# Node stage two moved into the last groups of the third edge pass, with edge-less nodes ranked first

## The reference

```
deg  = segment_sum(1, dst) + 1;  dinv = rsqrt(deg)
agg  = segment_sum((x * dinv)[src], dst) * dinv + x * dinv^2      # layer L2: the sum over neighbours
msg  = gelu(agg @ W + b)                                          # 128 x 128
x    = layernorm(x + msg)
# layer L3, per edge: gelu([x[src], x[dst], w] @ We1 + be1), summed over edges of one dst
t3   = x @ We1[0:128];   bd = x @ We1[128:256] + be1              # tables that the fourth pass gathers
```

## Time and profile before

| what | us |
|---|---|
| median of 3 runs | 10237.42 (10231.23 to 10249.54) |
| profiled execution, its span | 10211.6 |
| third pass: first gather after 5334, last add ends | 7567.98 |
| first gather of the fourth pass | 7690.86 |
| PE, DVE, ACT, POOL busy over the span | 51%, 51%, 23%, 60% |

### The profile page before, as it was taken

The page is one execution under the profiler, slowest core; times in us unless marked ns, Lnnn a source line. Parts: engine busy times, 40 slices in busy tenths (PEclk is TensorE's granted clock), DMA queues, the critical chain, the costliest instruction groups (busy, mean ns, idle before and its releaser), DMA issues. The chain is left out here.

```text
span 10211.6 us, 117807 instructions
## 1 busy us (share of the span) xinstructions
PE 5172.9 (51%) x26943; PEld 4434.7 (43%) x27385; DVE 5157.6 (51%) x11737; ACT 2350.8 (23%) x7991; POOL 6159.7 (60%) x6684
## 2 busy tenths in 40 slices
PE   1544444447365666666673323333345565666655
PEld 1434433435254555555552222222244555555553
DVE  4644544546466666666652222222245555555556
ACT  1212211224244444444460000000021111111114
POOL 5666666662566555555516666666656666666664
PEclk9556556667677777777786656555576766666677
DMA  4222222222444444444421111111123333333331
GB/s 110 46 46 47 46 46 46 47 46 86 100 101 99 99 98 98 98 98 98 99 68 47 46 47 46 47 46 46 46 62 109 100 101 101 102 100 102 101 100 43
DMA packets 869663, 769.76 MB, mean 75 GB/s; under 512 B 385028, under 2 KB 727929, under 8 KB 868606
## 3 DMA queue, kind: packets, MB, share of 16 engines
q0 software_dynamic: 230416, 528.66, 20.4%
q1 hardware_dynamic: 626235, 228.48, 9.4%
q10 hardware_dynamic: 12344, 5.06, 0.2%
HBM read 707.24 MB, written 54.30 MB: 75 GB/s over the span
## 5 line engine op out<-in xcount | busy, mean ns | idle before, releaser
L1007 POOL DMA_INDIRECT rows_h<-t_d,idx x1563 | 1482.3, 948 | 1024.9 <-issue 396.3
L581 POOL DMA_INDIRECT rows_sum<-t_d,idx x1563 | 1474.7, 944 | 962.8 <-issue 453.5
L581 POOL DMA_INDIRECT rows_mlp<-t_d,idx x1548 | 1468.7, 949 | 834.1 <-remote 419.0
L1007 POOL DMA_INDIRECT rows<-t_d,idx x1477 | 1396.7, 946 | 812.6 <-issue 409.7
L1152 PEld LDWEIGHTS pn_h<-S_h,rows_h 128*128 128x128 f32 x6252 | 1098.1, 260 | 258.5 <-issue 223.2
L1152 PE MATMUL pn_h<-S_h,rows_h 128*128 128x128 f32 x6252 | 1141.6, 348 | 124.8 <-issue 110.3
L1047 ACT ACTIVATE rows_h<-rows_h,wc_h 128x64 f32<-128x64 f32 x4688 | 1135.9, 334 | 17.1 <-issue 7.0
L772 DVE TENSOR_TENSOR big<-big,pn_sum 128x512 f32 x391 | 269.2, 689 | 1687.0 <-remote 1535.6
L620 PE MATMUL pre_mlp<-dw_mlp,ST_mlp 128*128 128x128 f32 x3126 | 674.5, 379 | 475.8 <-DVE ST_mlp L59 185.3
L627 PE MATMUL pn_sum<-zb_sum 128*128 128x512 bf16 x325 | 175.4, 540 | 1294.4 <-DVE big L772 1089.9
L620 PEld LDWEIGHTS pre_mlp<-dw_mlp,ST_mlp 128*128 128x128 f32 x3126 | 591.2, 280 | 528.5 <-issue 513.8
(11 more groups left out here) (361 smaller groups left out, 8634.5 us busy)
## 6 DMA issues: line engine op xcount, KB each, us to landing
dw_mlp<-bd_d SPq DMA_DIRECT2D x1563, 64.0 KB
frow_mlp<-t_d ACTq DMA_DIRECT2D x1920, 0.5 KB
frow_h<-t_d SPq DMA_DIRECT2D x1792, 0.5 KB
lrb_h<-lrrow_d SPq DMA_DIRECT2D x196, 128.0 KB
lrb_mlp<-lrrow_d SPq DMA_DIRECT2D x98, 256.0 KB
rows_h<-t_d,idx POOLq DMA_INDIRECT x1563
dw_h<-xp_d SPq DMA_DIRECT2D x1563, 3.0 KB
rows_sum<-t_d,idx POOLq DMA_INDIRECT x1563
```

The lines of the kernel that those rows point to most:

```text
L581: e.indirect_dma_start(rows[:, g % NR, j, :], None, table, bass.IndirectOffsetOnAxis(ap=idx[:, b, t:t + 1].bitcast(I32), axis=0)).then_inc ...
L1007: e.indirect_dma_start(rows[:, g % NR, j, :], None, table, bass.IndirectOffsetOnAxis(ap=idx[:, b16, t:t + 1].bitcast(I32), axis=0)).then_i ...
```

## The change

**Ranks.** Nodes without edges get the first ranks and nodes with edges end at rank NP - 1 = 12543, so that the last window ends at the end of `big`. The comparison that builds the prefix matrix is turned, offsets are taken from NP instead of from 0, and the bounds that go with register loads say NP in place of N. `big` becomes longer: RANKS is 13056 in place of 13016.

**One block for pass and node stage.** `edge_sum` takes the place of `edge_light("sum")` and `node2`. Gathers, hot, place and add are those of before. From group 368 (LAST) on, each engine does one step of the node stage behind each group: steps 0 to 22 inside the pass, 23 to 32 behind it.

- `project(u)` waits until the add of group 367 + u is done (`settled`), since with the new ranks all of unit u is final then.
- In the step s, PE runs place(368 + s), project(s), fill(s - 7), turn(s - 6); ACT turned(s - 6), normal(s - 5), bend(s), fill(s - 7) and, in some steps, deviate; DVE hot, add, message(s), settle(s - 1), fill(s - 8) and, in some steps, scale.
- pt and pg have one buffer each in place of two (PSUM holds pn as well). PE's fill(u) waits for ACT's and DVE's fill(u - 1).
- POOL's Newton steps are gone. ACT's `deviate` takes the square root of variance + eps for a run of units (7 runs of three, 2 of two units), and DVE's `scale` takes the reciprocal, in steps 4, 7, 10, 13, 16, 19, 22, 24 and 26.
- The last part of POOL is the clearing of half 1, behind all gathers; each memset waits only for project.

The weight loading at the start of the pass is the same instructions in the new function, and `edge_light` is still there for the fourth pass.

```diff
-RANKS = N + 4 * P + 4
+RANKS = NP + 4 * P
...
-        edge_light(nc, sb, "sum", t2_d, big, dict(consts, dn=dn, w=w, a=a), d)
-        node2(nc, sb, big, dinv, w, consts, a, d)
+        edge_sum(nc, sb, t2_d, big, dinv, dict(consts, dn=dn, w=w, a=a), d)
...
-            e.tensor_scalar(tri[:, :], iota[:, :], iotap[:, 0:1], None, ALU.is_gt)
+            e.tensor_scalar(tri[:, :], iota[:, :], iotap[:, 0:1], None, ALU.is_le)
...
-            e.tensor_scalar(bf[:, :], ct[:, :, 0], off[:, 0:1], -1.0, ALU.add, ALU.add)
+            e.tensor_scalar(bf[:, :], ct[:, :, 0], off[:, 0:1], float(NP), ALU.subtract, ALU.add)
...
-                e.tensor_copy(n["rb"][:, :], nump[0:1, 0:NT])
                 e.tensor_copy(off[:, :], nump[0:NT, P:P + 2])
                 e.drain()
+                e.tensor_scalar(n["rb"][:, :], nump[0:1, 0:NT], off[0:1, 1:2], float(NP), ALU.subtract, ALU.add)
...
-                e.tensor_scalar(away[:, :], away[:, :], off[:, 1:2], None, ALU.add)
-                e.tensor_scalar(pos[:, :], pos[:, :], -1.0, None, ALU.add)
+                e.tensor_scalar(pos[:, :], pos[:, :], off[:, 1:2], NP - 1.0, ALU.subtract, ALU.add)
...
+LAST = GR - UNITS + 2
+RUNS = [range(k, min(k + 3, 21)) for k in range(0, 21, 3)] + [range(21, 23), range(23, UNITS)]
+RUN = {u: k for k, run in enumerate(RUNS) for u in run}
+LATE = 5
...
+def settled(u):
+
+    return min(GR, -(-(TILES - NT + min(NT, 4 * u + 4)) // 4))
...
+        pn = [ps(f"pn{i}", [P, 512]) for i in range(2)]
+        pa, pt = [ps(f"pa{i}", U4) for i in range(2)], ps("pt", U4)
+        pg = ps("pg", [P, 4, 2, F])
...
+        turns = {u + LATE: u for u in range(UNITS)}
+        ends = {run[-1]: k for k, run in enumerate(RUNS)}
+        STEPS = UNITS + LATE + 3
...
+            def project(u):
+
+                t, n = unit(u)
+                e.wait_ge(s_add, settled(u))
+                if u == 0:
+                    e.wait_ge(s_pv, 4)
+                if u >= 2:
+                    e.wait_ge(s_z, u - 1)
...
+            def turn(u):
+
+                t, n = unit(u)
+                e.wait_ge(s_n, u + 1)
+                if u >= 1:
+                    e.wait_ge(s_xT, u)
...
+            def fill(u):
+
+                n = unit(u)[1]
+                e.wait_ge(s_xT, u + 1)
+                if u >= 1:
+                    e.wait_ge(s_ta, u)
+                    e.wait_ge(s_tb, u)
...
+            def after(step):
+
+                if step < UNITS:
+                    project(step)
+                if step - 2 in turns:
+                    fill(turns[step - 2])
+                if step - 1 in turns:
+                    turn(turns[step - 1])
+
+            for g in range(GR):
...
+                place(g, r0[4 * q:4 * q + 4])
+                if g >= LAST:
+                    after(g - LAST)
+            for step in range(GR - LAST, STEPS):
+                after(step)
...
+            def deviate(k):
+
+                t0, t1 = span(RUNS[k])
+                e.wait_ge(s_y, RUNS[k][-1] + 1)
+                e.activation(dev[:, t0:t1, :], mv[:, t0:t1, 1:2], ACT.Sqrt, bias=c["eps"][:, 0:1]).then_inc(s_dev, 1)
...
+            for step in range(STEPS):
+                if step - 1 in turns:
+                    turned(turns[step - 1])
+                if step in turns:
+                    normal(turns[step])
+                if step < UNITS:
+                    bend(step)
+                if step - 2 in turns:
+                    fill(turns[step - 2])
+                if step - 2 in ends:
+                    deviate(ends[step - 2])
...
+            def scale(k):
+
+                t0, t1 = span(RUNS[k])
+                e.wait_ge(s_dev, k + 1)
+                scalars(e, dev[:, t0:t1, :], mv[:, t0:t1, 0:1], rs[:, t0:t1, :], nm[:, t0:t1, :]).then_inc(s_rs, 1)
...
+            def after(step):
+
+                if step < UNITS:
+                    message(step)
+                if 0 <= step - 1 < UNITS:
+                    settle(step - 1)
+                if step - 3 in turns:
+                    fill(turns[step - 3])
+                if step - 2 in ends:
+                    scale(ends[step - 2])
+
+            hot(0)
+            for i in range(GR + 1):
+                if i + 1 < GR:
+                    hot(i + 1)
...
+                    add(g, r0[g % 16])
+                if LAST <= i < GR:
+                    after(i - LAST)
+            for step in range(GR - LAST, STEPS):
+                after(step)
```

More of the change, by code:

```diff
@@ L2059, in _ @@
         def _(e):
-            def clear(u):
+            for g in range(GR):
+                if g >= NR:
+                    e.wait_ge(s_mm, g - NR + 1)
+                b, q = divmod(g, NQ)
+                for j in range(SIZE[g]):
+                    t = 4 * q + j
+                    e.indirect_dma_start(rows[:, g % NR, j, :], None, table,
+                                         bass.IndirectOffsetOnAxis(ap=idx[:, b, t:t + 1].bitcast(I32), axis=0)
+                                         ).then_inc(s_g[g % NR], 16)
+            for u in range(UNITS):
                 t, n = unit(u)
                 e.wait_ge(s_A, u + 1)
[L2064 to L2097, removed]
+                e.memset(acc[:, 1, t * P:(t + n) * P], 0.0)
             e.drain()
@@ L2107, in project @@
                 for j in range(n):
[L2108 removed]
+                    last = e.matmul(pa[u % 2][:, j, :], acc[:, 1, (t + j) * P:(t + j + 1) * P], wt["wg"][:, :], start=True, stop=True)
                 last.then_inc(s_A, 1)
@@ L2172, in fill @@
                     e.wait_ge(s_o[u % 2], 32 * (u // 2))
[L2173 to L2183, removed]
+                e.copy(ta[u % 2][:, 0:n, :], pg[:, 0:n, 0, :]).then_inc(s_ta, 1)
@@ new lines, in _ @@
+            for i in range(3):
+                e.tensor_scalar(mask[:, 3 + i:4 + i], p9, float(i), None, ALU.is_equal)
+            e.drain()
+            e.tensor_tensor(mask[:, 1:2], mask[:, 0:1], mask[:, 2:3], ALU.add)
+            e.drain()
+            e.tensor_scalar(mask[:, 1:2], mask[:, 1:2], -1.0, 1.0, ALU.mult, ALU.add)
+            e.wait_ge(s_p, 2)
+            e.tensor_copy(wt["V"][:, :], pw[:, 1, :])
+            e.tensor_copy(v9[:, :], pw[0:9, 2, :])
+            e.drain().then_inc(s_pv, 1)
@@ new lines, in parts, with choose @@
+            def parts(x, out, n):
+                for i in range(3):
+                    e.tensor_copy(out[:, i, :], x)
+                    e.drain()
+                    if i < 2:
+                        e.tensor_tensor(x, x, out[:, i, :], ALU.subtract)
+                        e.drain()
+            def choose(out, p, m, n):
+                e.tensor_scalar(out, p[:, 0, :], mask[0:n, m:m + 1], None, ALU.mult)
+                for i in (1, 2):
+                    e.drain()
+                    e.scalar_tensor_tensor(out, p[:, i, :], mask[0:n, m + i:m + i + 1], out, ALU.mult, ALU.add)
+                e.drain()
@@ new lines, in _ @@
+            parts(degf[:, :], deg, NT)
+            e.drain().then_inc(s_pv, 1)
+            parts(v9[:, :], v9p, 9)
+            choose(v9r[:, :], v9p, 0, 9)
+            e.tensor_copy(wt["v9"][:, :], v9r[:, :])
+            e.tensor_tensor(bu2[:, :], bu2[:, :], be3[:, :], ALU.subtract)
+            e.drain()
+            parts(bu2[:, :], v9p[0:3, :, :], 3)
+            choose(v9r[0:3, :], v9p[0:3, :, :], 3, 3)
+            for j in range(4):
+                e.tensor_copy(wt["b3"][:, j, :], v9r[0:3, :])
@@ L2187, in message, with add @@
+            def add(g, r0):
+                e.drain()
+                e.wait_ge(s_mm, g + 1)
+                w = acc[:, 1, bass.ds(r0, 4 * P)]
+                e.tensor_tensor(w, w, pn[g % 2][:, :], ALU.add).then_inc(s_add, 1)
             def message(u):
```

189 lines of the change are left out of this document (139 added, 50 removed).

## The result

The changed kernel took 10,360.24 us (median of 5 runs, 10,324.36 to 10,386.77) against 10,237.42 before in the same comparison (10,219.41 to 10,251.98): ratio 1.0112, 95% interval 1.0097 to 1.0128. It is 122.8 us slower; 119 was forecast.

What follows compares the result with a forecast made beforehand. No engine was full in the third pass, but the added steps form a serial turn through PE and DVE. Terms 52 + 33 + 34 = +119 us gave 10,356 us, range 10,235 to 10,450.

Steps and rivals of the forecast that it cites:

- The ring: Interleaved steps: each plain step with a fill is one serial turn through PE and DVE, 8.26 us against a group's 4.20.
- message(0): First node-stage message on DVE: starts at 7473.4, after add 367 ends at 7471.47 and a 1.91 us project.
- steps 8 to 22: Node-stage steps inside the pass: five times (14.1 + 9.11 + 8.26) = 157.4 us at the high clock.
- the bare ring: Third pass and node stage at the high clock without late releases: next gather at 7743.3 against 7690.86, +52.4 us.
- Numbering at 0: Numbering edge-less nodes first: same instructions on the same shapes, cost 0, bounds under 1 us to either side.
- The clock: PE's low clock in the steps: one late step in three, +33 us, bounds 0 and +82.
- Late releases: Releases while gathers run beside the steps: 2.27 us per step, +34 us, bounds 0 and 126.
- Rival (c): Each project's release is as late as an add's, on top of the clock: +211, 10,448 us, chance 0.15.
- Sqrt: Nine runs on ACT: DVE waits behind ACT's step, a 1283 ns load and the Sqrt; such steps take 14.1 us.
- (b): Steps keep PE busy enough for a high clock and releases are prompt: +52, 10,290 us, chance 0.20.
- (d): The next step's fill finds tb done, so gain and loss cancel: within 20 us, chance 0.05.
- Rival (a): Steps fit within the group's time, so groups still end at about 7568: -61, 10,176 us, chance 0.12.

Runs made afterwards that it cites:

- first experiment: Kernel before the change with only the new numbering of nodes; 8520.89 us against 8520.55, ratio 1.0.
- experiment 11: Changed kernel with 16 added matmuls in each step that has a fill, ahead of PE's wait for tb; 10,192.1 us against 10,113.14, ratio 1.0070.
- fifth experiment: Changed kernel unaltered, run again beside its variants; 8612.88 us against 8519.23 for the kernel before, ratio 1.0107.
- third experiment: Changed kernel with Identity in place of Sqrt in the nine runs, so no table loads there; 8594.01 us, ratio 1.0084 to the kernel before.
- seventh: Changed kernel with DVE's tb first, PE's turn ahead of fill, and DVE's scale one step later, ahead of message; 8462.03 us, ratio 0.9932 to the kernel before.
- the fourth: Changed kernel with DVE's tb first in its step and PE's turn ahead of its fill; 8485.17 us, ratio 0.9957 to the kernel before.
- eighth experiment: Changed kernel with DVE order tb, scale, settle, message, PE's turn ahead of fill, ACT's fill ahead of bend; 8445.81 us against 8519.23, ratio 0.9913.

## Why the prediction was right

The ring was the right mechanism. That the sum came within 4 us of the measured loss is luck: two of its terms are wrong and their errors cancel. Each term, with the start of the third pass taken as common:

| term | forecast | measured |
|---|---|---|
| message(0) | 7473.4 + 45.0 = 7518.4 | 7533.7, +15.3 |
| steps 0 to 7 | 51.3 | 56.6, +5.3 |
| steps 8 to 22 | 157.4 | 192.4, +35.0 |
| message(23) to the next gather | 61.2 | 77.6, +16.4 |
| over the bare ring | 33 + 34 = 67 | 72.0 |

- *Numbering at 0*: right (first experiment).
- *The ring*: right. The chain tb, fill, turn, place, project, message is in the rows, the fill's 94 us of waiting on DVE's tb is its mark, and four calls in another place take it away. Its 8.26 us at the high clock were never seen bare; the nearest are the plain steps of 8.4 to 9.6 at a clock of 0.90 (experiment 11).
- *The clock*: mis-sized. The forecast had one late step in three, 33 in all; the excess over the bare ring outside message(0) is 5.3 + 35.0 + 16.4 = 56.7. Matmuls were slow in most steps (median 634 ns), as the ring itself makes PE pause 4 us each time. Holding the clock with other work gave back 25 of the 35 us in steps 8 to 22; of the 21.7 outside them, where fewer or no matmuls were added, it gave back 3.9 in the last part and nothing in steps 0 to 7. So the clock is shown for about half of this term, and for the rest it is argued.
- *Late releases*: mis-sized the other way, 34 forecast. They fell once, on message(0): add 367 ended 4.5 us earlier than forecast, and from its end to the message it took 21.7 us where 1.9 were forecast, 15.3 in all; of the later messages none waited for "remote". In the fifth experiment none fell at all, and the loss was 93.6. The reading behind this term was wrong. It took the 3.9 us that an add waits for "remote" as lateness, but where gathers run evenly the adds wait 1430.4 us in all, 3.7 each, released by PE (last part): groups come every 5.0 us there, as four gathers do. So most of that wait is the gathers' pace; some 257 of the 1687 us of idle time are more than that. The add at 7540.61, which waits 0.20, is not behind the last gather either, which starts at 7556.7. Rival (c) is out: the ring is the same with and without gathers.
- *Sqrt*: the scale step's surplus of 5.8 us was about right (5.1 to 6.5 over the step ahead of it). I charged load, Sqrt and ACT's step in front alike; taking the loads away gives back 2.2 us a run (third experiment), and moving the scale one step later takes the whole surplus away, with the loads kept (seventh, in the fourth's order).
- *Rivals (b) and (d)*: the clock stayed low (0.72), and the ring was not looser than read (the fill waited 4 us for tb in each step).
- *Rival (a)* failed at the point that it named: the ring needed 10 to 17 us, the group gave 4.2 to 5.7. The eighth experiment, at 5.5 us a step (82.26 over 15), is close to rival (a) made true: its last gather starts at 6263.0, against 6261.2 in the kernel with all steps behind the pass (both passes start at 4311), so its steps hold the gathers up by no more than 2 us.

The Trainium skill's drain ("ScalarE: Activation LUTs", section What ACT_TABLE_LOAD costs, about 1380 ns a switch besides the load) does not show: the copy ends at 7623.19, the load starts at 7623.20 and ends at 7624.48, the Sqrt starts at 7624.50. The measurement decides; the 10,377 by the Trainium skill's figure would have been further off (measured 10,360) than 10,356.

## What to carry to other kernels

When two stages are interleaved and a double buffer is given up for it, write down the ring that one turn makes through each engine's order and compare it with the pace of the loop it is to hide in; idle shares of 60% say nothing on that. First do what another engine waits for (here tb ahead of message), last what waits for another engine, and use a result of a third engine one step after it was ordered. A ring that makes TensorE pause cost twice here, by the pause and by the clock behind it (25 of 192 us in steps 8 to 22).

## What had not been expected of the hardware

The same kernel takes 10,237, 10,113 or 8,520 us in different comparisons. Where it is long, POOL pauses some 4.5 us after every 24 gathers and adds wait for "remote"; where it is short, the same adds wait for PE only (numbering alone, groups):

```profile
L772 DVE TENSOR_TENSOR big<-big,pn_sum 128x512 f32 x391 | 269.3, 689 | 1430.4 <-PE pn_sum L640 1430.0 <-issue 0.4
...
L581 POOL DMA_INDIRECT rows_sum<-t_d,idx x1563 | 1474.7, 944 | 683.6 <-issue 476.0 <-ACTq L460 207.5
```

and gathers start every 1.25 us without a pause. A gather itself is 944 ns in both. In the long run the third pass, first to last gather, takes 272 us more (2221.9 against 1949.8), and POOL's waits for "remote" in it add up to 286.6. What makes the pauses, and why message(0) started 19.6 us after its matmuls had ended in the record (7514.14 to 7533.73), stays open. POOL, too, went on only at 7534.75, after 4.53 us of the same kind. In the kernel without gathers beside the steps no add or message there waits for "remote", so such waits come beside gathers; which way the one causes the other is not shown.
